# A top-3 mixture that stores its last products in list order and gathers each token's three rows at the end

## The reference, cut to what matters

```
h = _apply_mixture(x_flat, dw1, W1)      # 3 of 12 experts per token, 256 -> 1024
h = gelu(h)
y = _apply_mixture(h, dw2, W2)           # again 3 of 12, by another router, 1024 -> 256
y = y + dw3 @ b2
x = x + y
```

## Time and profile before

| | us |
|---|---|
| median of 3 runs | 1221.43 (1219.93 to 1226.13) |
| span of the profiled execution | 1216.9 |
| median less that span | 4.5 |

### The profile page before, as it was taken

One profiled execution on the slowest core, in us unless ns is written; L12 is line 12 of the kernel. 1 busy time (PEld: TensorE's weight loads), 2 busy tenths in 40 slices (PEclk: granted clock), 3 DMA queues, 4 the chain that ended last, 5 costly groups with the idle time before them and its releaser, 6 DMA issues.

```text
span 1216.9 us, 19171 instructions
## 1 busy us (share of the span) xinstructions
PE 1094.3 (90%) x6013; PEld 817.2 (67%) x6013; DVE 552.3 (45%) x1120; ACT 420.3 (35%) x833; POOL 381.8 (31%) x421
## 2 busy tenths in 40 slices
PE   7999899998999999999399999998677888888885
PEld 4888744888998878887244443444566777776773
DVE  4988766764444446776872501333122211111114
ACT  1566544321112225664244432332222232222220
POOL 0221100000220011011154434552666646665650
PEclk8999999998999999999599999998898899999998
DMA  7000130004980029001155578997778865444437
GB/s 208 2 0 0 33 139 1 1 1 161 345 286 9 0 66 382 27 0 47 37 180 200 186 211 295 349 364 276 249 253 278 269 201 179 134 131 142 132 121 281
DMA packets 93410, 187.89 MB, mean 154 GB/s; under 512 B 14109, under 2 KB 34575, under 8 KB 93340
## 3 DMA queue, kind: packets, MB, share of 16 engines
q1 hardware_dynamic: 65346, 109.45, 25.4%
q0 software_dynamic: 23696, 73.69, 19.6%
q10 hardware_dynamic: 4298, 3.81, 1.0%
HBM read 133.56 MB, written 55.44 MB: 155 GB/s over the span
## 4 chain that ended last, share of the span: by engine, by line
PE 40%; issue 4%; DMA 4%; DVE 2%; another core or an unknown queue 2%; ACT 1%; SPq 0%; POOL 0%; POOLq 0%; DVEq 0%; ACTq 0%
PE f_psY L2089 18%; PE f_psH L2046 15%; PE f_psV L2072 4%; DMA W<-in_f_W1T 2%; DMA W<-p_d 2%; PE f_psT L2034 1%; ACT a_W L2146 1%; DVE W L1650 1%; PE f_psV L83 1%; DMA shared<-h_d,f_half_toks 0%; PE f_psH L1929 0%; PE f_psV L1662 0%; SPq L2343 0%; DVE f_xTk L2268 0%
## 5 line engine op out<-in xcount | busy, mean ns | idle before, releaser
L2089 PE MATMUL f_psY<-W,a_W 128*128 x944 | 240.7, 401 | 57.4 <-issue 35.6
L2089 PEld LDWEIGHTS f_psY<-W,a_W 128*128 128x128 f32 x944 | 179.4, 200 | 87.0 <-issue 65.4
L2046 PE MATMUL f_psH<-W,f_xTk 128*128 x472 | 215.5, 596 | 5.7 <-ACT shared L2141 2.0
L2046 PEld LDWEIGHTS f_psH<-W,f_xTk 128*128 128x128 f32 x472 | 84.1, 190 | 96.0 <-issue 95.6
L2146 ACT ACTIVATE a_W<-f_psV 128x512 f32<-128x512 f32 x118 | 70.0, 598 | 155.8 <-PE f_psV L2072 94.8
L2141 ACT ACTIVATE shared<-f_psH 128x512 f32<-128x512 f32 x118 | 70.4, 597 | 142.1 <-PE f_psH L2046 109.5
L1692 POOL DMA_INDIRECT W<-p_d,f_rows x96 | 95.0, 989 | 64.7 <-issue 24.7
L1692 POOL DMA_INDIRECT shared<-h_d,f_half_toks x90 | 87.6, 974 | 85.4 <-DMA p_d<-shared 25.6
L2246 DVE TENSOR_SCALAR a_W<-W,f_wt 128x512 f32<-128x512 f32 x32 | 15.9, 496 | 204.7 <-DMA W<-p_d,f_rows 147.6
L2268 DVE TENSOR_TENSOR f_xTk<-f_psY,f_xTk 128x256 f32<-128x256 f32 x52 | 21.7, 424 | 144.1 <-PE f_psY L2089 112.5
L1692 POOL DMA_INDIRECT a_W<-xn_d,f_toks x59 | 57.6, 975 | 88.9 <-PE f_psT L2034 54.3
(11 more groups left out here) (299 smaller groups left out, 1867.8 us busy)
## 6 DMA issues: line engine op xcount, KB each, us to landing
p_d<-shared SPq DMA_DIRECT2D x118, 256.0 KB
W<-in_f_W1T SPq DMA_DIRECT2D x24, 512.0 KB, 8.8
W<-in_f_W2T SPq DMA_DIRECT2D x24, 512.0 KB
m_wg<-in_m_Wg SPq DMA_DIRECT2D x16, 512.0 KB, 4.0
m_wu<-in_m_Wu SPq DMA_DIRECT2D x16, 512.0 KB, 5.2
m_wd<-in_m_Wd SPq DMA_DIRECT2D x16, 512.0 KB, 6.1
h_d<-a_W SPq DMA_DIRECT2D x32, 256.0 KB
W<-p_d SPq DMA_DIRECT2D x16, 384.0 KB, 9.2
```

The costliest lines, as they stand in the source:

```text
L2046: mm = pe.matmul(psH[:, n % 2, :], xTk[:, i, k, :], W1[c][:, e, k, :], start=k == 0, stop=k == KD - 1)
L2089: mm = pe.matmul(psY[:, n % 2, 0:D], hT[:, m % 2, k, :], W2[c][:, e, k, :], start=k == 0 and not (whole and c == 1), stop=k == KQ - 1 and ...
```

## The change

The router's table of list places is used for the last mixture too, so `dest` is not needed:

- `y_part[:, i]` is stored in list order to tile i of `p2_d` by a plain transfer on SP's queue, each as soon as its result is ready; `p2_d` shrinks to LT * 128 rows. The 59 scatters on POOL are gone.
- At the end POOL waits for all 59 stores and issues 48 gathers, one for each token tile i and choice k, of 128 rows of 1 KB each, by `rows[:, 1, k, i]`. The 16 plain loads on SP are gone. Each token tile has a semaphore of its own, and PE and DVE wait for all three gathers of a tile.
- `at_tile` loses its second digit: the 48 matmuls of the second list have 60 columns instead of 120, DVE issues 16 instructions fewer for them (L2232) and 5 fewer in `found_tokens`, one copy (`rows[:, 1]`) is added after `lists`. The load of `spare` and its wait are gone.

The diff, cut to its core:

```diff
-    p2_rows = nc.dram_tensor("p2_d", (B * N * TOP + LT * P, D), F32, kind="Internal").ap()
-    p2_d = p2_rows[0:B * N * TOP, :].rearrange("(i p k) d -> i p k d", k=TOP, p=P)
+    p2_rows = nc.dram_tensor("p2_d", (LT * P, D), F32, kind="Internal").ap()
+    p2_d = p2_rows.rearrange("(i p) d -> i p d", p=P)
...
-                rows = sb(st, "f_rows", [P, TOP, TT], U32)
+                rows = sb(st, "f_rows", [P, 2, TOP, TT], U32)
...
-                        one.step(dve.scalar_tensor_tensor(own[:, :], found[:, 0:LT], 0.0, spare[:, :],
-                                                          ALU.is_equal, ALU.mult))
-                        one.step(dve.scalar_tensor_tensor(pair[:, :], pair[:, :], float(TOP), found[:, LTE:LTE + LT],
-                                                          ALU.mult, ALU.add))
-                        one.step(dve.tensor_tensor(pair[:, :], pair[:, :], own[:, :], ALU.add))
-                        one.step(dve.tensor_copy(pairi[:, 0], pair[:, :]))
-                        one.step(dve.tensor_copy(dest[:, :], pairi[:, 0]))
...
-                            def scatter(n):
-                                i = turns[n].tile
-                                pool.wait_ge(yo_ready, n - FIRST + 1)
-                                pool.indirect_dma_start(p2_rows, bass.IndirectOffsetOnAxis(ap=dest[:, i:i + 1], axis=0),
-                                                        y_part[:, i, :], None
-                                                        ).then_inc(yo_stored_diag if i < DIAGS else yo_stored, 16)
...
                             for n in range(FIRST, len(turns)):
                                 hidden(n)
-                                if n >= FIRST + DEEP - 1:
-                                    scatter(n - DEEP + 1)
-                            for n in range(len(turns) - DEEP + 1, len(turns)):
-                                scatter(n)
+                            pool.wait_ge(yo_stored_diag, 16 * DIAGS)
+                            pool.wait_ge(yo_stored, 16 * (LT - DIAGS))
+                            for i in range(TT):
+                                for k in range(TOP):
+                                    fetch(pool, last[:, i, k, :], p2_rows, rows[:, 1, k, i:i + 1], last_ld[i])
...
-                                    add_tokens(pe, j, 2, psF, at_used)
+                                    add_tokens(pe, j, psF, at_used)
...
-                                pe.wait_ge(last_ld[i % (TT // 2)], 16 * (i // (TT // 2) + 1))
+                                pe.wait_ge(last_ld[i], 16 * TOP)
...
                             lists(dve, one, psN)
+                            one.step(dve.tensor_copy(rows[:, 1], pki[:, :, :]))
...
-                                dve.tensor_scalar(at_tile[:, i % AR, :, 0, :], at_hit[:, i % AR], tokid[:, i:i + 1], None, ALU.mult)
-                                dve.tensor_tensor(at_tile[:, i % AR, :, 1, :], at_hit[:, i % AR],
-                                                  iota[:, 0:TOP].unsqueeze(2).to_broadcast([P, TOP, LTE]), ALU.mult)
+                                dve.tensor_scalar(at_tile[:, i % AR], at_hit[:, i % AR], tokid[:, i:i + 1], None, ALU.mult)
...
-                            sp.wait_ge(yo_stored_diag, 16 * DIAGS)
-                            sp.wait_ge(yo_stored, 16 * (LT - DIAGS))
-                            for i in range(TT):
-                                s = i % (TT // 2)
-                                wait(sp, last_ld[s], 16 * (i // (TT // 2)))
-                                sp.dma_start(last[:, i], p2_d[i]).then_inc(last_ld[s], 16)
+                            for n in range(FIRST, len(turns)):
+                                i = turns[n].tile
+                                sp.wait_ge(yo_ready, n - FIRST + 1)
+                                sp.dma_start(p2_d[i], y_part[:, i, :]
+                                             ).then_inc(yo_stored_diag if i < DIAGS else yo_stored, 16)
```

More of the change, by code:

```diff
@@ L1550, in top3_mixture @@
                 tokid = sb(st, "f_tokid", [P, TT])
-                spare = sb(st, "f_spare", [P, LT])
-                dest = sb(st, "f_dest", [P, LT], U32)
                 pair = sb(st, "f_pair", [P, LT])
@@ L1569, in top3_mixture @@
                 at_hit = carve(AR * TOP * LTE // 2).bitcast(F16).rearrange("p (a k n) -> p a k n", a=AR, k=TOP)
-                at_tile = carve(AR * TOP * LTE).bitcast(F16).rearrange("p (a k d n) -> p a k d n", a=AR, k=TOP, d=2)
+                at_tile = carve(AR * TOP * LTE // 2).bitcast(F16).rearrange("p (a k n) -> p a k n", a=AR, k=TOP)
                 below = carve(P)
@@ L1658, in match_row, with add_tokens @@
                         pmod[:, :, i:i + 1].to_broadcast([P, TOP, P]), ALU.is_equal)
-                def add_tokens(pe, i, digits, found, at_used):
+                def add_tokens(pe, i, found, at_used):
                     for k in range(TOP):
-                        mm = pe.matmul(found[:, 0:digits * LTE], at_row[:, i % AR, k, :], at_tile[:, i % AR, k, 0:digits, :],
+                        mm = pe.matmul(found[:, 0:LTE], at_row[:, i % AR, k, :], at_tile[:, i % AR, k, :],
                                        start=i == 0 and k == 0, stop=i == TT - 1 and k == TOP - 1)
@@ L1814, in top3_mixture @@
                     diag_ready = sem("f_diag_ready")
-                    last_ld = [sem(f"f_last_ld{i}") for i in range(TT // 2)]
+                    last_ld = [sem(f"f_last_ld{i}") for i in range(TT)]
                     last_mm = sem("f_last_mm")
@@ L1827, in route_sync @@
                         sp.dma_start(tokid[:, :], t["c_tokid"]).then_inc(ld, 16)
-                        sp.dma_start(spare[:, :], t["c_spare"]).then_inc(ld, 16)
                         clear_stale(sp)
@@ L1864, in route_vector @@
                             norm_in(u)
-                        dve.wait_ge(ld, 16 * 4)
+                        dve.wait_ge(ld, 16 * 3)
                         one.step(dve.tensor_tensor(
@@ L1895, in route_scalar @@
                                        ).then_inc(z_copied, 1)
-                        act.wait_ge(ld, 16 * 4)
+                        act.wait_ge(ld, 16 * 3)
                         for i in range(TT):
@@ L1899, in route_scalar @@
                             wait(act, r_at_used, i - AR + 1)
-                            act.activation(at_tile[:, i % AR, :, 0, :], at_hit[:, i % AR], ACT.Copy, scale=tokid[:, i:i + 1]
+                            act.activation(at_tile[:, i % AR], at_hit[:, i % AR], ACT.Copy, scale=tokid[:, i:i + 1]
                                            ).then_inc(tile_ready, 1)
@@ L1905, in route_gpsimd @@
                         pool.memset(ones_b[:, :], 1.0).then_inc(consts, 1)
-                        pool.wait_ge(ld, 16 * 4)
+                        pool.wait_ge(ld, 16 * 3)
                         pool.tensor_copy(below_b[:, :], below).then_inc(consts, 1)
@@ L1952, in route_tensor @@
                             pe.wait_ge(tile_ready, i + 1)
-                            add_tokens(pe, i, 1, psF, r_at_used)
+                            add_tokens(pe, i, psF, r_at_used)
                     with nc.Block() as block:
@@ L1967, in three @@
                                     wait(pool, hs_ready, u - GR + 1)
-                                fetch(pool, g[u // TT][:, u % GR, k, :], p1_rows[c], rows[:, k, i:i + 1], g_ld[u % GR])
+                                fetch(pool, g[u // TT][:, u % GR, k, :], p1_rows[c], rows[:, 0, k, i:i + 1], g_ld[u % GR])
                             def all_sums(c):
@@ L2191, in _ @@
                             dve.sem_inc(owner_ready, 1)
-                            one.step(dve.tensor_copy(rows[:, :, :], pki[:, :, :]))
+                            one.step(dve.tensor_copy(rows[:, 0], pki[:, :, :]))
                             pick(dve, one, 1, 0, 0, TT)
@@ L2272, in weighted @@
                                 if k == 0:
-                                    dve.wait_ge(last_ld[i % (TT // 2)], 16 * (i // (TT // 2) + 1))
+                                    dve.wait_ge(last_ld[i], 16 * TOP)
                                 else:
@@ L2437 @@
         "c_tokid": flip(np.arange(1, 1 + B * N, dtype=np.float32).reshape(B * NT, P)),
-        "c_spare": np.arange(B * N * TOP, B * N * TOP + LT * P, dtype=np.float32).reshape(LT, P).T.copy(),
         "c_ident": np.eye(P, dtype=np.float32),
```

## The result

| | us |
|---|---|
| kernel before, median of 4 runs | 1222.64 (1219.93 to 1226.13) |
| changed kernel, median of 4 runs | 1232.07 (1228.34 to 1232.16) |
| ratio | 1.0078, 95% interval 1.0047 to 1.0109 |
| span of the profiled execution, before and after | 1216.9, 1230.1 |

The change makes the kernel slower by 0.8%, some 9 us, where I had forecast 27 us. The time of the changed kernel's profiled execution is known, 1232.07 us, so only 2.0 us lie around a span. The profile of before, taken as 1216.9 + 2.0 = 1218.9 us, was therefore one of the shorter executions, and the two spans differ by more (13.2 us) than the medians (9.4 us).

What follows compares the result with a forecast made beforehand. PE was taken to bound the products, with unexplained idle gaps, and DMA the end. Losing 39.6 us at the end, gaining 12.5 in the products and 0.4 by the second list gave 1243.6, plus 4.5 around it about 1248; range 1234 to 1264.

Steps and rivals of the forecast that it cites:

- the relief of PE: Products without scatters on POOL: half of PE's 25.8 us idle time goes, 12.5 us gained; bounds 0 and 25.8.
- seam and end: From the last result to the end of the span: seam 0, gathers and what follows them 39.6 us slower.
- What bounds the kernel: Last mixture's products bound by PE with a loss of unnamed cause, POOL second to look at; DMA engines bound the end.
- a coincidence of place: Products: POOL's queue taken for 134 of 161 us where PE loses time, not yet counted as a cause.
- they go altogether: Rival for the products: all 25.8 us of PE's gaps vanish, since POOL's full queue matters; 1234.8 us, chance 0.23.
- The seam: Between last result and first gather: gather starts at about 1190.0 us, where SP's load started before; worth 0.
- The gathers: 48 at the end, issued singly by POOL: 47 steps of 1.257 us, 59.1 us, last landing in 2.7 us.
- The pauses of POOL: Rival for the 48 gathers: five or six pauses, 10 us more; about 1258 or 1271 us, chance 0.05.
- a share near a quarter of 0.85: Sign for the last 60 us: DMA share expected there while POOL is the bound.
- Behind the last gather: End of the kernel: 2.7 us landing plus 4.7 us for PE, DVE, store and slow matmuls.
- The second list: Its 48 matmuls with 60 columns instead of 120 gain 0.4 us; bounds 0 and 2.7.
- Faster by overlapping issues: Rival for the end: gathers run at the earlier 311 GB/s, not by issue pitch; 1208 us, chance 0.03.

Runs made afterwards that it cites:

- the other chips: Three chips on which the experiments ran: the unchanged kernel before takes 1158.6 to 1161.3 us there, the changed kernel 1198.04 us (ratio 1.0326).
- 30 extra scatters: Changed kernel plus 30 scatters to a table nobody reads, one in every second of the last 59 turns: 1197.86 us, 1.0333 to the kernel before.
- the first chip: Chip assumed for the first pair of kernels, with no number on record: kernel before 1222.64 us, changed kernel 1232.07 us.

## Why the prediction was wrong, point by point

I forecast 1248 us, range 1234 to 1264; the median is 1232.07, below the range. The direction was right, the size was not. The 16.0 us between forecast and result divide as follows: the relief of PE was 35.9 us and not 12.5 (-23.4); seam and end cost 44.4 - 0.3 = 44.1 us and not 39.6 (+4.5); the stretch ahead of the turns grew by 5.1 us where I had -0.4 (+5.5); 2.0 us lie around the span and not 4.5 (-2.5). Together -15.9. (Half of the 25.8 us of idle time is 12.9 and not 12.5; the slip is worth 0.4 us.)

**What bounds the kernel: right for the most part.** PE with a loss that comes with the scatters, then the end. I set POOL's queue at 134 of 161 us as a coincidence of place. On the other chips it is the cause: there it is 139.5 of 143 us, and 30 extra scatters instead of 59 cost next to nothing.

**The relief of PE: the failed step.** It failed twice. First the bound. "What the relief gives PE is bounded by 0 ... and 25.8 us" took PE's idle time for all that PE lost. But a PE that is shown as busy can get less done as well. From 1012 to 1187 us the kernel before had 772 matmuls in 149.53 us of busy time, 0.194 us each; after, 768 took 139.00 us, 0.181 each. That difference, 772 x 0.0127 = 9.8 us, is loss inside the busy time. 25.8 + 9.8 = 35.6 us, the 35.9 that were won. About half of the 9.8 us is PE's clock, which the earlier trace rows gave as 0.97 and of which I made nothing. Three stretches of 5 us hold it, each with a group of products that stands behind a gap (the columns are those of the earlier trace rows):

```profile
1022.00:1027.00 5.00, 4.27 (x14) 3.46 (x15) 0.85 (x2) 1.24 (x3) 2.63 (x3) 0.66 0.34 107
1082.00:1087.00 5.00, 3.42 (x12) 2.80 (x13) 0.42 (x1) 1.77 (x4) 2.95 (x3) 0.74 0.34 112
1102.00:1107.00 5.00, 5.00 (x21) 4.10 (x20) 0.65 (x3) 1.55 (x4) 3.04 (x4) 0.71 0.24 81
```

These 47 matmuls took 12.69 us, 4.2 us more than at 0.181 each. PE had been idle for 1.91, 3.68 and 2.53 us ahead of these groups; behind a gap of 3.20 us, at 1137.59, the clock stayed at 1.00.

Most of the rest is overlap that each gap undoes. Without a gap the products start 0.44 us after the start of their transposes, which last 0.60, and the next transposes start 1.72 us after the products (1131.62, 1132.06 and 1133.78 us in the rows below). At a gap the whole 0.60 us pass as busy time, and then 1.82 until the next transposes. That is 0.26 us for each gap, some 4 us for the other 15, an estimate.

The page of before could have told it, in the stretch that I used only for its idle time: in the earlier trace rows, 127 matmuls in 23.00 us are 0.181 each, 704 in 136.44 are 0.194.

Second the choice: I took the middle of the bounds, for the number of transfers halved. All of the loss went. The case "they go altogether" had this right, with its 1234.8 us from the same small bound; with 35.9 in place of 25.8 and the rest of its sum unchanged it would have said 1224.7.

This also bounds what the experiments prove. On three chips POOL's load explains the loss of PE by scatters as a bound on POOL's queue, worth 5 us. On the first chip the loss was over seven times as large, and POOL's queue was not full (134 of 161 us). What stood in that trace was late signals. The waits of the kernel before from 1012 to 1187 us (total us, times, longest):

```profile
ACT a_W L2146 <- remote: 33.8, 12, 5.9
DVE f_xTk L2268 <- remote: 22.2, 6, 5.7
DVE f_xTk L2265 <- remote: 5.4, 1, 5.4
POOL shared L1692 <- remote: 3.7, 2, 2.0
```

I had read PE's waits and not those of the engines that answer it. One such place in order of time, PE and then ACT: PE's transposes L2072 start at 1133.78 us, ACT sees them at 1136.79, and PE stands still until 1137.59, 0.2 us after ACT's answer is complete.

```profile
1131.62 0.60 PE L2072 MATMUL f_psV<-ident,sel 128*128 128x128 f32 x4
1132.06 1.89 PE L2089 MATMUL f_psY<-W,a_W 128*128 x8
1133.78 0.60 PE L2072 MATMUL f_psV<-ident,sel 128*128 128x128 f32 x4
1137.59 1.99 PE L2089 MATMUL f_psY<-W,a_W 128*128 x8 [3.20 <-issue]
1139.41 0.60 PE L2072 MATMUL f_psV<-ident,shared 128*128 128x128 f32 x4
```

```profile
1136.79 0.60 ACT L2146 ACTIVATE a_W<-f_psV 128x512 f32<-128x512 f32 x1 [4.85 <-remote]
```

Over the two traces of that chip the late signals go with POOL's busy share (sums of all "remote" waits in a stretch):

| stretch, us | kernel | POOL busy | late, us |
|---|---|---|---|
| 560 to 740 | before, after | 0.35, 0.35 | 0, 0 |
| 740 to 840 | before, after | 0.47, 0.46 | 1.6, 5.6 |
| 845 to 987 | before, after | 0.66, 0.66 | 48.6, 55.0 |
| 1012 to 1187, scatters | before | 0.62 | 65.1 |
| 987 to 1010 | before | 0.36 | 1.5 |
| 1190 to 1217, plain loads | before | 0 | 0 |
| 1017 to 1156, no scatters | after | 0.35 | 0 |
| 1158 to 1230, 48 gathers | after | 0.63 | 19.9 |

None of the twelve traces from the other chips has a single such wait, at shares of POOL up to 0.75. So on the first chip dense indirect transfers and late signals of PE come together in every stretch of these two traces. That the one causes the other there is likely but only argued. Why it happened there and not on the other chips stays open. At one place the rows tell a held PE from a held signal: in the end of the changed kernel PE starts the matmuls of tile 13 at 1213.27 us, 10.0 us before DVE is released for tile 11, so there PE went on and only the signal was late. For the turns that is not known.

**The seam: right.** Forecast as worth 0; 2.75 us became 2.45.

**The gathers: right.** 47 steps of 1.257 us forecast, 1.257 measured, with rows half as large as those it was read from. The last one landed some 2.8 us after its start (1218.00 to 1220.82), forecast 2.7. The pauses of POOL did not come. The Trainium skill (DMA: Bandwidth & Descriptors, Issuing engines are not separate DMA queues) calls the time to initiate a DMA "usually small relative to the DMA itself"; here 48 x 128 KB took 59 us by issue alone, and the DMA share was 0.39. I had named a share near a quarter of 0.85 as a sign; it was nearly half of it. By my own pitch, 128 KB in 1.257 us are 104 GB/s, a third of the 311 GB/s before, so the sign was set too low.

**Behind the last gather: too small by 4.7 us.** Forecast 7.4 us, measured 12.1. The forecast was 2.7 for the landing, 1.6 for PE, 2.5 for DVE and the store as in the earlier trace rows, and 0.6 for slow matmuls. Measured were 2.8 for the landing, 2.93 for PE, 4.05 from PE's recorded end to DVE's at 1227.80, and 2.3 for the store. PE's part is its clock: the groups come some 7.5 us apart and run at the lower level (the granted clock is 0.50 from 1220 to 1224 us), so the price was 1.4 us more than in the earlier trace rows, and I had allowed 0.6. DVE's part is the late signals; on another chip, without them, it was 0.5 us, but there the store took 3.9, so that 10.4 us remained in all.

**The second list: not to be seen.** Forecast -0.4 us; the first gather of hidden rows came 2.3 us later, about as much as the most that it could have gained, and the runs do not tell the two apart.

**Rivals.** Faster by overlapping issues, and the rule behind it: excluded, the pitch stands. Slower by over 0.5% had a chance of 0.96 and came in, with the interval starting at 0.5%.

No version of these beats the kernel before with the right rows in place. The stores in list order were worth 5.6 us on one of the other chips, where alone they were measured, but the 48 gathers that they need cost 42.

## What to carry to other kernels

Indirect transfers are priced by their number on the issuing engine, and the price shows only where it is not hidden: on the other chips 59 scatters beside PE cost 5 us (36 on the first), and 48 gathers with nothing beside them cost 42. Before bounding what a relief can give, divide the busy time of the bound engine by its instructions, in the troubled stretch and in a clean one, and look at its granted clock; and read the waits of the engines that answer it. Look at the kernel before on the chip of each experiment first, since the same change was +0.8% where it was first measured and +3.3% on another chip.

## What the runs showed of the hardware

- The same kernel took 1222.6 us in the first measurement and 1158.6 to 1161.3 on three chips later. All but 2.6 of the 58.9 us between two traced spans lie behind the first gather of hidden rows at 840 us, in stretches dense with indirect transfers.
- An indirect transfer costs POOL 1.25 us (0.95 and a pause of 0.30) for 128 rows, of 1 KB or 2 KB alike. It can be longer when DVE adds from the on-chip memory at the time: in the run where DVE does all the sums, 13 of the 48 gathers took 1.08 to 1.15 us, all of them overlapped by a sum, and the others at most 0.97. Over all 48 the mean is 994 ns instead of 953. The Trainium skill (GPSIMD Engine Reference, 1. Specifications) says that GpSimd's path to that memory is shared with VectorE, with contention when a DVE instruction has two inputs there; the sums of L2250 have, and the trace agrees: none of the 18 gathers that no sum overlaps took more than 0.95 us.
- Behind three of 18 gaps in the turns of the kernel before, PE's granted clock fell to its lower level: 0.66, 0.74 and 0.71 in the 5 us that follow, with PE idle for 1.91, 3.68 and 2.53 us before; after a gap of 3.20 us it did not.
- The last store took 2.1, 2.3, 3.9 or 5.7 us from the last result to the end of the span, at the same size of 128 KB; the runs do not say by what.
